# Loading attention operands through a second DMA queue, with sources repeated inside one transfer

## What is computed

```python
q = (x @ Wq) ; k = (x @ Wk) ; v = (x @ Wv)          # 16 heads of 16; 4 groups of 16
att = einsum('bhqd,bhkd->bhqk', q, k) * scale + alibi + causal
y = einsum('bhqk,bhkd->bhqd', softmax(att), v) @ Wo
x = layernorm(x + y)
x = layernorm(x + shared_expert(x) + routed_expert(x))
```

## Time and profile before

| | us |
|---|---|
| median of 3 runs | 586.63 |
| lowest, highest | 584.7, 589.06 |
| the profiled execution | 584.91 |
| span of its trace | 583.1 |
| TensorE busy | 534.2 (92%) |
| VectorE busy | 303.5 (52%) |

### The profile page before, as it was taken

One profiled execution on the slowest core, in us unless ns is written; L12 is line 12 of the kernel. 1 busy time (PEld: TensorE's weight loads), 2 busy tenths in 40 slices (PEclk: granted clock), 3 DMA queues, 4 the chain that ended last, 5 costly groups with the idle time before them and its releaser, 6 DMA issues.

```text
span 583.1 us, 7872 instructions
## 1 busy us (share of the span) xinstructions
PE 534.2 (92%) x2602; PEld 263.4 (45%) x2602; DVE 303.5 (52%) x630; ACT 223.8 (38%) x455; POOL 124.2 (21%) x165
## 2 busy tenths in 40 slices
PE   5958999999999999998788789999999999999992
PEld 2323333333333333332115575546664656566651
DVE  1469988888788888885004655122221424243432
ACT  2320266667576666666561012110012222222220
POOL 4511000000000000000000110973003454545453
PEclk9977699999999999999967898999999999999997
DMA  7598410404040404063882540032013122222220
GB/s 230 151 249 237 80 35 3 107 2 97 13 89 21 88 21 89 21 257 142 296 231 78 172 163 2 0 127 91 0 54 101 55 75 62 76 61 73 65 54 29
DMA packets 41344, 55.32 MB, mean 95 GB/s; under 512 B 5706, under 2 KB 29646, under 8 KB 41271
## 3 DMA queue, kind: packets, MB, share of 16 engines
q1 hardware_dynamic: 29490, 31.33, 20.3%
q10 hardware_dynamic: 8840, 15.36, 8.1%
q0 software_dynamic: 2976, 8.14, 4.6%
HBM read 36.12 MB, written 18.51 MB: 94 GB/s over the span
## 4 chain that ended last, share of the span: by engine, by line
PE 82%; DVE 7%; DMA 3%; ACT 2%; ACTq 1%; issue 1%; POOL 1%; SPq 1%; POOLq 0%; DVEq 0%
PE ps L679 14%; PE ps L508 12%; PE ps L483 11%; PE ps L599 10%; PE ps L499 10%; PE ps L698 7%; PE ps L610 5%; DVE mx L847 5%; PE ps L571 3%; PE ps L498 2%; PE ps L485 2%; PE ps L690 2%; PE ps L453 2%; PE ps L588 1%; DMA cb<-in_cb 1%
## 5 line engine op out<-in xcount | busy, mean ns | idle before, releaser
L847 DVE TENSOR_REDUCE mx<-ps 128x1 f32<-128x512 f32 (+4 forms) x312 | 186.2, 644 | 40.5 <-PE ps L485 25.5
L766 ACT ACTIVATE probs<-ps 128x512 f32<-128x512 f32 x288 | 153.4, 603 | 99.0 <-PE ps L499 91.1
L483 PE MATMUL ps<-qk_or_dn 103*128 103x512 bf16 (+3 forms) x384 | 122.6, 345 | 10.7 <-DMA qk_or_dn<-qparts 6.2
L499 PE MATMUL ps<-qk_or_dn 103*128 103x512 bf16 x288 | 102.3, 386 | 1.5 <-ACT probs L766 1.3
L679 PE MATMUL ps<-wgu,tmp 128*128 x184 | 82.9, 593 | 0.1
L483 PEld LDWEIGHTS ps<-qk_or_dn 103*128 103x128 bf16 x384 | 38.3, 100 | 92.6 <-DVE mx L847 69.0
L508 PE MATMUL ps<-probs,Vs 128*32 128x512 f32 x576 | 77.6, 611 | 0.7 <-ACT probs L766 0.7
L485 PE MATMUL ps<-cb 128*128 128x128 bf16 x256 | 53.6, 233 | 0.0
L1028 DVE TENSOR_TENSOR tmp<-tmp,ps 128x512 f32<-128x512 f32 x23 | 15.8, 687 | 65.0 <-PE ps L679 65.0
L679 PEld LDWEIGHTS ps<-wgu,tmp 128*128 128x128 f32 x184 | 33.2, 190 | 33.3 <-issue 33.3
L698 PE MATMUL ps<-qk_or_dn,tmp 128*128 x184 | 43.6, 380 | 0.8 <-ACT tmp L828 0.8
(11 more groups left out here) (108 smaller groups left out, 478.8 us busy)
## 6 DMA issues: line engine op xcount, KB each, us to landing
wgu<-in_gu ACTq DMA_DIRECT2D x8, 1024.0 KB, 5.3
qk_or_dn<-qparts SPq DMA_DIRECT2D x48, 128.0 KB
yT<-yU SPq DMA_DIRECT2D x16, 256.0 KB, 2.1
qk_or_dn<-in_dn SPq DMA_DIRECT2D x8, 512.0 KB, 8.1
qparts<-tmp SPq DMA_DIRECT2D x8, 384.0 KB, 2.7
tmp<-xs SPq DMA_DIRECT2D x23, 128.5 KB, 2.2
tmp<-yT SPq DMA_DIRECT2D x34, 64.0 KB
xs<-rows ACTq DMA_DIRECT2D x1, 2056.0 KB
```

Source lines behind the costliest of these rows:

```text
L483: mm = pe.matmul(o, q, K6[k][0:KROWS, k0:k0 + w], start=True, stop=not masked)
L499: pe.matmul(o, K6[k][0:KROWS, kb * P:(kb + 1) * P], Q6[k][0:KROWS, :, qi * P:(qi + 1) * P], start=kb != qi, stop=True).then_inc(s_st, 1)
L766: act.activation(probs[:, 4 * (s % 3) + p, :], ps[:, 4 + (4 * s + p) % SB, :], ACT.Exp, scale=SCALE).then_inc(s_exp, 1)
L847: dve.tensor_reduce(o, ps[:, a_bank(u, t), 0:nh * w].rearrange("p (h w) -> p h w", h=nh), AX.X, ALU.max).then_inc(s_amax, 1)
```

## The change

The loads of units 0 and 1 (`load_unit_q`, `load_unit_k`) are issued from ScalarE's queue, ahead of its copies of jobs 6 and 8; their heads are issued by SyncE at the start. `load_unit_q` issues 3 transfers in place of 6, here and in the loop: each reads one part and repeats it in the source with a step of zero, for 3, 2 and 1 blocks of 16 partitions (`RUNS` lists part, first block and number of blocks: (0, 0, 3), (1, 3, 2), (2, 5, 1)). For this Wq's columns are reordered on the host, so that a channel's four heads are neighbours and a partition's 8 KB are contiguous in DRAM. `FIRST_A` becomes 6. `cf` and `cb` have semaphores of their own; job 1 waits only for the key and value weights. SyncE loads `cb` last. The six late loads are issued by GpSimd after `max_rows` of unit 0 has landed.

```diff
-FIRST_A = 8
+FIRST_A = 6
...
+        def load_unit_q(queue, u, i):
+            for part, s, n in RUNS:
+                r = ROW0 + s * D
+                heads = qparts_d[part:part + 1, bass.ds(u * HG * D, HG * D), :].rearrange(
+                    "o (d h) t -> o d (h t)", h=HG)
+                queue.dma_start(Q6[i][r:r + n * D, :, :].rearrange("p h t -> p (h t)"),
+                                heads.broadcast_to([n, D, HG * T])).then_inc(s_qk[i], 16)
+
+        def load_unit_k(queue, u, i):
+            for _, s, n in RUNS:
+                r = ROW0 + s * D
+                queue.dma_start(K6[i][r:r + n * D, :], kparts_d[0:n, bass.ds(u * D, D), :]).then_inc(s_qk[i], 16)
...
-            def load_unit_q(u, i):
-                for s, part in enumerate(Q_PART):
-                    r = ROW0 + s * D
-                    sp.dma_start(Q6[i][r:r + D, :, :], qparts_d[part, bass.ds(u * HG * D, HG * D), :]
-                                 .rearrange("(h d) t -> d h t", h=HG)).then_inc(s_qk[i], 16)
...
             load_x(1)
-            sp.dma_start(cf[:], cf_d).then_inc(s_w0, 16)
-            sp.dma_start(cb[:], cb_d).then_inc(s_w0, 16)
-            load_x(2)
-            load_x(3)
+            sp.dma_start(cf[:], cf_d).then_inc(s_cf, 16)
             for i in range(STEP):
...
+            for u in range(2):
+                load_unit_head(u, u)
+            load_x(2)
+            load_x(3)
+            sp.dma_start(cb[:], cb_d).then_inc(s_cb, 16)
             for n in range(NJ):
...
-                if n == UNIT0_JOBS:
...
-                    load_unit_head(0, 0)
-                    load_unit_k(0, 0)
-                if n == UNIT0_JOBS + 1:
-                    load_unit_q(0, 0)
-                if n == FIRST_A:
-                    load_unit_head(1, 1)
-                    load_unit_k(1, 1)
-                if n == FIRST_A + 1:
-                    load_unit_q(1, 1)
...
                 if n == 1:
-                    pe.wait_ge(s_w0, 16 * 4)
+                    pe.wait_ge(s_w0, 16 * 2)
...
                 if n == FIRST_A + 1:
                     pe.wait_ge(s_one, 32 * STEP)
+                    pe.wait_ge(s_cb, 16)
                     pe.wait_ge(s_qk[0], S_QK)
...
+                if n == UNIT0_JOBS + 2:
+                    for i in range(3):
+                        act.wait_ge(s_pw[i], 16 * ((UNIT0_JOBS + 2 - i) // 3))
+                    load_unit_k(act, 0, 0)
+                    load_unit_q(act, 0, 0)
+                if n == UNIT0_JOBS + 4:
+                    load_unit_k(act, 1, 1)
+                    load_unit_q(act, 1, 1)
                 act.activation(parts0[n % 3][0:m, 0, :], ps[0:m, 4 + n % 4, :], ACT.Copy).then_inc(s_ph, 1)
...
             for u in range(2):
                 values(u, u)
+            pool.wait_ge(s_mrow, 48)
+            for dst, src, done in ((x_all[:], x_d, s_x), (wo[:], wo_d, s_wo), (rt[:], rt_d, s_wo),
+                                   (wsg[:], sg_d, s_wsh), (wsu[:], su_d, s_wsh), (wsd[:], sd_d, s_wsh)):
+                pool.dma_start(dst, src.rearrange("(k p) n -> p k n", p=P)).then_inc(done, 16)
```

More of the change, by code:

```diff
@@ L27 @@
 ROW0 = M_ROWS + AL_ROWS
[L28 to L31, removed]
+RUNS = ((0, 0, 3), (1, 3, 2), (2, 5, 1))
+KROWS = ROW0 + D * sum(n for _, _, n in RUNS)
 SCALE = float(D) ** -0.5
@@ L227, in layer @@
         ones = cb[:, CB_ONE:CB_ONE + P]
-        s_wq, s_w0, s_x, s_wo, s_wsh, s_wgu, s_wdn = (
-            sem(n) for n in ("s_wq", "s_w0", "s_x", "s_wo", "s_wsh", "s_wgu", "s_wdn"))
+        s_wq, s_w0, s_cf, s_cb, s_x, s_wo, s_wsh, s_wgu, s_wdn = (
+            sem(n) for n in ("s_wq", "s_w0", "s_cf", "s_cb", "s_x", "s_wo", "s_wsh", "s_wgu", "s_wdn"))
         s_xT = [sem(f"s_xT{i}") for i in range(NCH)]
@@ L258, in layer @@
         s_out = [sem(f"s_out{i}") for i in range(NZ)]
-        S_QK = 16 * (2 + len(Q_PART) + len(K_RUNS))
+        S_QK = 16 * (2 + 2 * len(RUNS))
         def a_bank(u, t):
@@ L279, in load_unit @@
                 load_unit_head(u, i)
-                load_unit_q(u, i)
-                load_unit_k(u, i)
+                load_unit_q(sp, u, i)
+                load_unit_k(sp, u, i)
             def load_unit_head(u, i):
@@ L372, in _ @@
                              parts0[n % 3][0:m, :, :]).then_inc(s_pw[n % 3], 16)
-                if n == UNIT0_JOBS:
-                    for i in range(3):
-                        sp.wait_ge(s_pw[i], 16 * ((UNIT0_JOBS + 2 - i) // 3))
-                    load_unit_head(0, 0)
-                    load_unit_k(0, 0)
-                if n == UNIT0_JOBS + 1:
-                    load_unit_q(0, 0)
-                if n == FIRST_A:
-                    load_unit_head(1, 1)
-                    load_unit_k(1, 1)
-                if n == FIRST_A + 1:
-                    load_unit_q(1, 1)
             for i in range(3):
@@ L460, in values @@
                     pe.wait_ge(s_vev, c)
+                else:
+                    pe.wait_ge(s_cf, 16)
                 for t in range(TPC):
@@ L727, in put_values @@
                 ins.then_inc(s_vev, 1)
-            later_loads = [(x_all[:], x_d, s_x), (wo[:], wo_d, s_wo), (rt[:], rt_d, s_wo), (wsg[:], sg_d, s_wsh),
-                           (wsu[:], su_d, s_wsh), (wsd[:], sd_d, s_wsh)]
             for n in range(NJ):
@@ L737, in _ @@
                     act.wait_ge(s_pw[n % 3], 16 * (n // 3))
+                if n == UNIT0_JOBS + 2:
[6 more added lines that the diff above has]
+                    load_unit_q(act, 1, 1)
                 act.activation(parts0[n % 3][0:m, 0, :], ps[0:m, 4 + n % 4, :], ACT.Copy).then_inc(s_ph, 1)
-                i = 2 * (n - FIRST_A - 1)
-                for dst, src, done in later_loads[i:i + 2] if i >= 0 else []:
-                    act.dma_start(dst, src.rearrange("(k p) n -> p k n", p=P)).then_inc(done, 16)
                 if k == 2:
@@ L1179 @@
     arrays = {
-        "x": x, "xT": np.ascontiguousarray(x.T), "wq": L0_attn_Wq, "wk": L0_attn_Wk, "wv": L0_attn_Wv,
+        "x": x, "xT": np.ascontiguousarray(x.T), "wq": np.asarray(L0_attn_Wq).reshape(C, NG, HG, D).transpose(0, 1, 3, 2).reshape(C, NH * D),
+        "wk": L0_attn_Wk, "wv": L0_attn_Wv,
         "wo": np.asarray(L0_attn_Wo).reshape(NH, D, C).transpose(1, 0, 2).reshape(NH * D, C),
```

## The result

The changed kernel is slower: 624.9 us (623.18 to 625.48) beside 587.5 us in the same comparison, a ratio of 1.0637 with a 95% interval of 1.0589 to 1.0686. The forecast was 594.3 us, range 586 to 603. Its direction was right; the kernel lost about five times what was forecast. The span of the profiled execution grew from 583.1 to 623.5 us.

A forecast was written before the change was run, and what follows sets the result against it. The prediction took the front, up to the first exponential, as the bound: unit 0's landing 5.0 us later, two more VectorE jobs 2.2 and a gap 0.5, together 7.7 us, giving a median of 594.3 us, range 586 to 603.

The forecast's parts named there:

- what bounds the kernel: Whole kernel: only the front has something to give; a front ending x us later makes the kernel x us longer.
- the mechanism: Unit loads: a transfer with 3 or 2 copies leading runs on 3 or 2 DMA engines, 14.7 us a unit.
- what VectorE has left: Front, behind unit 0's landing: five jobs instead of three, 2.2 us, plus one more gap of about 0.5 us.
- The path from the split to the first exponential: End of the front, from VectorE's last tile to the first exponential: unchanged at 7.4 us.
- the cover of ScalarE's issues: Front: unit 1's load issues, 3.6 us on ScalarE ahead of job 8's copy, are covered and cost nothing.
- The 0.67 us of `cb`: Start of the front: job 1 no longer waits for `cb`, so ScalarE reaches the new loads at 21.6 us.
- the front's duration: Unit 0's loads: 14.7 us at the busiest engine plus 2.1 us of stores; landing at 39.1 us, 5.0 later.
- The loop ... cost nothing, but that is a thin cover: Loop loads: 14.7 us within 16.1 us available, hidden by 1.4 us in five units, so no cost.
- the loop begins to wait: Rival, chance 0.23: below 21 GB/s at the busiest engine, loads come too late in units 1 to 5; 597 to 612 us.
- the late weights: Six late loads on GpSimd from about 75 us: cost nothing unless they hold up a unit's load.
- 27 us of GpSimd at that price: Late loads' issue time on GpSimd: some 3,600 rows at 0.96 us for 128 rows, while it has nothing else to do.
- 8 us of slack: Unit 0: unit 2's load has about 23 us, so it can bear 8 us of sharing engines with the late weights.

The follow-up runs named there:

- rows outermost: Changed kernel with the 16 rows outermost and copies or parts inside in the sources of Q and K loads; 586.29 us against 586.71, ratio 0.9998.

## Why the prediction was right and wrong

**Right: what bounds the kernel, and the mechanism.** The width of the transfer was read from two rows of the loop, and it holds: share 0.13 and 0.21 in the changed kernel, 1.0 with rows outermost, and the loss gone with it. The Trainium skill's rule on a leading zero-stride broadcast ("DMA: Bandwidth & Descriptors", "Rules for kernel authors") gives the same result, and this case's trace agrees: 0.21 with three copies, 0.13 with two. One slip in the working: 338 kB at each of two engines are two thirds of the 982 kB that were spread over sixteen, not half. Another: SyncE had nine load issues for a unit, not eight; nothing hung on it.

**Right, with some luck: what VectorE has left.** 2.7 us forecast, 2.7 measured (30.3 against 27.6). Some 0.8 us of it is half clock: TensorE's first job behind the landing took 2.81 us where rows outermost took 2.03, and VectorE's gap there is 1.69 us against 0.90. With rows outermost the term is 1.9 us, with `FIRST_A` = 6 alone 3.5, so the agreement to a tenth is chance. The path from the split to the first exponential came out right, unchanged at 7.4, and so did the cover of ScalarE's issues: VectorE has no gap on ScalarE behind the landing. The 0.67 us of `cb` showed (job 0 and job 1 in one run) but did not reach ScalarE at job 6: 22.35 us, not 21.6.

**Off in size: the front's duration.** Landing 41.5 us, forecast 39.1, just above the bounds of 36 to 41.3. Of the 2.4 us 0.75 is the start. The rest lies in the line at the two engines: I had added the stores' bytes there at the same rate (2.1 us) and the whole K part at 3.0 us, and it took longer; how it divides is not shown. The front cost 10.1 us where 7.7 were forecast.

**Wrong: "The loop ... cost nothing, but that is a thin cover".** This is the step that failed. I took 0.35 us to the first bytes, a figure for which no row stands, and 23 GB/s, the rate of K's short runs, and got 15.05 us from the issue, against the 16.5 there. It took 19.1. For five units I then wrote zero. A cover of 1.4 us on a term of 14.7 us taken from another transfer's rate is not a cover; the rival "the loop begins to wait" had 0.23 and is what happened. An issue-to-start time of 19.1 us is 338 kB at 17.7 GB/s over all of it, so of that rival's prices the upper one fits, 2.7 us in a unit at 18 GB/s, and the 0.5 us at 20.4 GB/s does not. Its 612 us are still 13 below the result: it left out the wait in unit 0 (below) and the half clock behind the waits, 4.1 us.

**Wrong: the late weights, "27 us of GpSimd at that price".** The price came from indirect transfers of 128 rows. The plain ones took 0.73 to 1.38 us whatever their size, so all 3.8 MB came at once, beside unit 2's load. I gave this load 8 us of slack; 240 kB for each engine at its 20 GB/s are 12 us. The two numbers stood in the text and were not set against each other. It cost 10.7 us.

Together: 10.1 + 10.7 + 17.6 = 38.4 us, where 7.7 + 0 + 0 were forecast.

**Open.** Why a unit's load takes 18 to 19 us in the loop and not 15. Part of it is the start: Q is issued at 125.79 us, and from 126 to 128 the load moves 20 GB/s where it then moves 61, some 1.3 us lost by an estimate from these windows. The rest is rate, 61 GB/s for three engines, 20 each; in the front three moved 66. What slows them is not shown: whether they read the same rows is unsettled, and the order of K and Q changes the wait more than the duration.

## What to carry to other kernels

Look at the outermost dimension of a DMA's source before its bytes: here three copies outside and sixteen rows inside ran on three engines, sixteen rows outside and three copies inside on all of them, with the same bytes and the same number of transfers, and the difference was 6% of the kernel. If a narrow transfer must stay, sum the bytes at its busiest engine, with everything else that goes through that engine meanwhile, and set it against the time until its use in every pass of a loop, not only in the front. Treat a cover that is smaller than the error of its largest term as no cover, and give it a price. Before moving loads to a time when an engine has nothing to do, ask which other transfer is under way there.

## What I had not expected of the hardware

- The length of one wait does not tell whether the clock falls behind it. In a loop in which TensorE is otherwise busy, waits of 2.93, 2.32, 2.76 and 2.78 us were followed by 3.4 us at a granted clock of 0.50 and one of 2.71 us was not; in the kernel with the repeated source alone one of 1.93 us was and one of 2.29 us was not. Shortening five waits by some 1.6 us and unit 0's by 3.3 us, with K first, brought 14 us.
- With all sixteen engines at work, the transfers into 48, 32 and 16 partitions together moved 181 to 221 GB/s, those into 16 partitions alone 150. The first read 8 KB runs for Q, the second runs of 2 KB, so this does not show which of the two differences counts.
- Two engines alone moved 53 to 55 GB/s in the front, about 27 GB/s each, more than the 22 that three had there (share 0.21, 66 GB/s) and the 20 that three had in the loop (share 0.21, 61 GB/s).
- Plain transfers issued by GpSimd cost it 0.73 to 1.38 us each, from 8 KB to 2 MB.
